# A recurrent block with a mixture-of-experts gate: biases put into PSUM by ScalarE, silu and half-tanh on ScalarE, experts in pairs, weights loaded in three groups

## What is computed

```python
xn = layernorm(x)
# the recurrent branch, on every second token of xn
xs = xn[:, ::2];  xs = xs * rsqrt(mean(xs**2) + 1e-6) * g_norm
x_proj, gate = split(xs @ w_in.T + b_in)
h = tanh(h * A + x_proj_t[:, None] * Bm)        # 2048 steps, h is (4, 512, 64)
y_t = h @ Cm.sum(0) + Dv * x_proj_t
s = repeat((y * silu(gate)) @ w_out.T + b_out, 2)
# the expert branch, on every token it needs (64 at a time per batch row)
spikes = sigmoid(xn @ W_enc + b_enc)            # 512 -> 1024
cont = spikes @ W_s2c + b_s2c                   # 1024 -> 64
gate2 = top-2 of softmax(cont @ Wr + br), renormalised      # 8 experts
eo = sum_e gate2_e * (relu(cont @ W1_e + b1_e) @ W2_e + b2_e)
spikes2 = sigmoid(eo @ W_c2s + b_c2s)           # 64 -> 1024
g = silu(layernorm(spikes2 @ W_dec + b_dec) * ln_g + ln_b)
out = x + s * g
```

## Time and profile before

| | |
|---|---|
| median of 3 runs | 6344.98 us |
| the profiled execution, its own time | 6343.27 us |
| its span, first to last instruction | 6341.6 us |
| PE busy | 6147.9 us, 97% |
| DVE busy | 5732.7 us, 90% |
| POOL busy | 5613.0 us, 89% |
| ACT busy | 3988.1 us, 63% |
| mean granted TensorE clock | 0.988 |
| DMA, mean over the span | 106 GB/s |

### The profile page before, as it was taken

How to read it: one execution, slowest core, us unless ns; L and a number is a source line. 1 busy time by engine, 2 the same in 40 slices (tenths; PEclk the granted TensorE clock), 3 DMA queues, 4 the chain that set the end, 5 groups by cost and what they waited for, 6 DMA issues and landing times.

```text
span 6341.6 us, 89178 instructions
## 1 busy us (share of the span) xinstructions
PE 6147.9 (97%) x29376; PEld 3202.8 (51%) x29376; DVE 5732.7 (90%) x10060; ACT 3988.1 (63%) x8390; POOL 5613.0 (89%) x3276
## 2 busy tenths in 40 slices
PE   5999999999999999999999999999999999999998
PEld 3555545555555455455554554555545545555554
DVE  4999999999999999999999999999999999999997
ACT  3666666666666666666666666666666666666665
POOL 4988989989889889899898898998988989989987
PEclk9999999999999999999999999999999999999999
DMA  5444444444434444444344444443444444444443
GB/s 144 104 110 99 110 105 104 110 102 107 110 99 110 105 103 110 102 107 112 97 110 106 103 113 102 105 113 95 109 108 102 114 101 106 112 96 110 109 102 80
DMA packets 157799, 672.95 MB, mean 106 GB/s; under 512 B 45589, under 2 KB 46613, under 8 KB 91799
## 3 DMA queue, kind: packets, MB, share of 16 engines
q1 hardware_dynamic: 157336, 667.24, 42.5%
HBM read 616.73 MB, written 50.33 MB: 105 GB/s over the span
## 4 chain that ended last, share of the span: by engine, by line
PE 91%; DVE 3%; POOL 3%; ACT 1%; issue 1%; SPq 1%; DMA 0%; POOLq 0%; DVEq 0%
PE bank L844 17%; PE bank L793 14%; PE ps_y L760 14%; PE ps_acc L856 9%; PE ps_acc L899 7%; PE bank L899 7%; PE bank L780 7%; PE bank L920 3%; PE bank L878 3%; PE bank L832 2%; POOL u L498 1%; PE bank L891 1%; PE ps_acc L891 1%; PE ps_acc L805 1%; PE ps_acc L878 1%
## 5 line engine op out<-in xcount | busy, mean ns | idle before, releaser
L498 POOL TENSOR_TENSOR u<-xb,bt 128x1024 f32<-128x1024 f32 x2048 | 4831.7, 2367 | 535.2 <-DVE ps_z L996 521.3
L600 ACT ACTIVATE h<-ps_z 128x512 f32<-128x512 f32 x4096 | 2377.1, 602 | 1280.0 <-DVE ps_z L996 1208.3
L990 DVE TENSOR_TENSOR ps_z<-h,ps_A 128x512 f32<-128x512 f32 x4096 | 2673.9, 691 | 416.0 <-ACT h L600 369.5
L996 DVE TENSOR_TENSOR ps_z<-ps_z,u 128x512 f32<-128x512 f32 x4096 | 2660.6, 691 | 8.7 <-POOL u L498 8.7
L844 PE MATMUL bank<-wide,w 65*128 65x256 f32 x4096 | 1138.8, 403 | 7.6
L760 PE MATMUL ps_y<-h,c_wide 128*32 128x512 f32 x8192 | 986.5, 599 | 0.0
L844 PEld LDWEIGHTS bank<-wide,w 65*128 65x128 f32 x4096 | 698.9, 189 | 454.6 <-issue 320.2
L793 PE MATMUL bank<-xnT,w_enc 128*128 128x256 f32 x4096 | 920.9, 383 | 6.5 <-ACT wide L623 6.5
L793 PEld LDWEIGHTS bank<-xnT,w_enc 128*128 128x128 f32 x4096 | 769.7, 190 | 213.0 <-issue 106.1
L681 ACT ACTIVATE hT<-bank 128x512 f32<-128x512 f32 x1024 | 604.1, 598 | 384.0 <-PE bank L844 366.6
L856 PE MATMUL ps_acc<-hT,w 128*64 128x256 f32 x4096 | 668.0, 404 | 6.7
(11 more groups left out here) (107 smaller groups left out, 4295.7 us busy)
## 6 DMA issues: line engine op xcount, KB each, us to landing
xb<-x_proj_scratch SPq DMA_DIRECT2D x2048, 256.0 KB, 4.5
xbuf<-in_L_attn_x SPq DMA_DIRECT2D x256, 128.0 KB
xres<-in_L_attn_x SPq DMA_DIRECT2D x512, 64.0 KB
out<-g SPq DMA_DIRECT2D x256, 128.0 KB
x_proj_scratch<-xp SPq DMA_DIRECT2D x256, 64.0 KB
w_in<-in_L_attn_w_in SPq DMA_DIRECT2D x1, 2048.0 KB
w_enc<-in_L_ffn_W_enc SPq DMA_DIRECT2D x1, 2048.0 KB
w_dec<-in_L_ffn_W_dec SPq DMA_DIRECT2D x1, 2048.0 KB
```

The costliest lines, as they stand in the source:

```text
L498: pool.tensor_tensor(u[:, tau % 2, :, :], xt, bt[:, :, :], ALU.mult).then_inc(u_ready, 1)
L600: act.activation(h[:, tau % RING, f, :], ps_z[:, f, :], ACT.Tanh).then_inc(h_ready, 1)
L990: dve.tensor_tensor(ps_z[:, f, :], h[:, (tau - 1) % RING, f, :], ps_A[:, f, :], ALU.mult).then_inc(m_done, 1)
L996: dve.tensor_tensor(ps_z[:, f, :], ps_z[:, f, :], u[:, tau % 2, f, :], ALU.add).then_inc(z_ready, 1)
```

## The change

- **Biases by ScalarE.** The three one-row matmuls of N=512 (decode twice, fin_out) go. ACT copies the bias, spread over 128 rows, into the bank (`dec_seed`, `out_seed`), and the matmuls add to it. The router's two bias matmuls and two copies go as well: Wr is turned into 64 columns of differences between experts, with the identity behind them, and one matmul for each half of the tokens makes both; one bias row of 256 columns is written before (`controller`).
- **Decode's layer norm.** W_dec and b_dec are centred once at the start, so that no mean is needed; ACT's Square with a sum gives the variance, and DVE's statistics, aggregates and centring go.
- **Sigmoids become tanh(x/2)**, with the affine part folded into the weights at the start. **Silu** runs on ACT alone, and POOL's three products go.
- **Routing** takes six smaller steps on DVE in place of eight; ACT's copy of the logits goes. The scale chain of the input norm is three small ACT and four small POOL operations in place of eight on POOL.
- **Experts in pairs**: two ups, then two downs, with four buffers for the relu's output in place of two.
- **Loads** in three groups on two queues: SyncE's (first) and ACT's (early, late), each waited for where it is needed. Preparing the weights is added at the start.
- Slots of the tables are moved throughout; `y` number 6 now stands between the two decodes.

The diff, cut to its core:

```diff
-PE_EXPERTS = (19, 19, 19, 19, 19, 19, 19, 19, 19, 19, 19, 20, 22, 22, 24, 28, 28)
...
+PE_EXPERTS = (19, 19, 19, 19, 19, 20, 22, 24, 28)
...
+        hidden = [hT[:, 0, :], hT[:, 1, :], conte_flat[:, 0:2 * T2], conte_flat[:, 2 * T2:4 * T2]]
...
+                sp.dma_start(dst, src).then_inc(first_loaded, 16)
...
-            def dec_silu(blk, q):
-                pool.wait_ge(g_sigmoid, 2 * blk + q + 1)
-                pool.tensor_tensor(g[:, q, :], g[:, q, :], sg[:, :], ALU.mult).then_inc(sg_used, 1)
...
+                act.wait_ge(p_stats_done, 4 * blk + 4)
+                act.activation(p_var[:, 0, :], p_mv[:, :, 1], ACT.Identity, bias=ln_eps[:, :])
+                act.activation(p_var[:, 1, :], p_mv[:, :, 1], ACT.Identity, bias=both_eps[:, :], scale=1.0 + RMS_EPS)
+                act.activation(p_mean[:, :], p_mv[:, :, 0], ACT.Copy, scale=-1.0).then_inc(p_moments, 1)
...
-            def gate_sig(blk, par):
+            def gate_silu(blk, par):
                 wait_drained(act, proj_fill(blk, FILL_WIN + 1))
-                if not is_first(blk):
-                    act.wait_ge(sg_used, sg_number(blk, None))
-                act.activation(sg[:, :], gt[:, par, :], ACT.Sigmoid).then_inc(gate_sigmoid, 1)
-            def sigmoids(src, k, bias):
+                act.activation(gt[:, par, :], gt[:, par, :], ACT.Silu).then_inc(gate_opened, 1)
+            def half_tanhs(src, k, bias):
                 for half in range(2):
                     m = 2 * k + half
                     ins = act.activation(wide[:, m, :], src[:, T2 * half:T2 * half + T2],
-                                         ACT.Sigmoid, bias=bias[:, m:m + 1])
+                                         ACT.Tanh, bias=bias[:, m:m + 1], scale=0.5)
...
+            def dec_seed(blk, q):
+                if q == 0:
+                    wait_drained(act, (blk, C2S_FILL[1]))
+                else:
+                    act.wait_ge(acc_drained, 2 * blk + 1)
+                act.activation(dec_out[q][:, :], b_dec_all[:, :], ACT.Copy).then_inc(dec_seeded, 1)
+            def out_seed(blk):
+                if is_first(blk):
+                    act.wait_ge(late_loaded, LATE)
+                wait_free(act, fin_fill(blk, FILL_FIN + 1))
+                act.activation(bank[1][:, :], b_out_all[:, :], ACT.Copy).then_inc(out_seeded, 1)
+            def dec_square(blk, q):
+                wait_dec_filled(act, blk, q)
+                if not (is_first(blk) and q == 0):
+                    act.wait_ge(d_stats_done, 2 * blk + q)
+                act.activation(squares[:, :], dec_out[q][:, :], ACT.Square,
+                               accum_out=d_ss[:, q:q + 1]).then_inc(d_stats_done, 1)
+            def dec_silu(blk, q):
                 wait_dec_drained(act, blk, q)
-                act.wait_ge(sg_used, sg_number(blk, q))
-                act.activation(sg[:, :], g[:, q, :], ACT.Sigmoid).then_inc(g_sigmoid, 1)
+                act.activation(g[:, q, :], g[:, q, :], ACT.Silu).then_inc(g_silu, 1)
...
+            load_early(w_enc[:, :, :], W_enc.rearrange("(k p) n -> p k n", p=P))
+            load_early(w_dec[:, :, :], W_dec.rearrange("(k p) n -> p k n", p=P))
+            load_early(w_s2c[:, :, :], W_s2c.rearrange("(k p) n -> p k n", p=P))
...
+            load_late(w_1[0:M, :, :], W1.rearrange("e m h -> m e h"))
...
+            act.wait_ge(first_loaded, FIRST)
...
+            act.wait_ge(early_loaded, EARLY)
...
+            act.wait_ge(weights_shaped, 1)
+            act.activation(w_dec_shift[:, :], w_dec_sum[:, :], ACT.Copy, scale=-0.5 / D).then_inc(weights_shaped, 1)
+            act.activation(w_s2c[:, :, :], w_s2c[:, :, :], ACT.Copy, scale=0.5)
...
+            act.wait_ge(weights_shaped, 2)
+            for k in range(KH):
+                ins = act.activation(w_dec[:, k, :], w_dec[:, k, :], ACT.Identity, bias=w_dec_shift[:, k:k + 1], scale=0.5)
+            ins.then_inc(weights_shaped, 1)
+            gate_silu(0, 0)
+            act.wait_ge(columns_summed, 1)
+            act.activation(cont_bias[0:M, :], ps_acc[0:M, 8:9], ACT.Identity, bias=cont_bias[0:M, :]).then_inc(biases_shifted, 1)
+            act.wait_ge(biases_shifted, 2)
...
+                pe.matmul(ps_acc[:, T2:T2 + 2 * (E * E + M)], ones[96:97, :], br_row, start=True, stop=True)
                 for k in range(KH):
                     half = k % 2
                     ins = pe.matmul(contT_acc[M * half:M * half + M, :], w_s2c[:, k, :], wide[:, k, :],
-                                    start=(k < 2), stop=(k >= KH - 2))
+                                    start=False, stop=(k >= KH - 2), skip_group_check=True)
...
-                    pe.matmul(logit_acc[:, q, :], ones[64:65, :], bias_rows[64:65, 0:E], start=True, stop=False)
-                    pe.matmul(logit_acc[:, q, :], tokens, w_r[:, :], start=False, stop=True)
-                    ins = pe.matmul(cont_acc[:, q, :], tokens, ident_2[:, :], start=True, stop=True)
+                    ins = pe.matmul(routed[:, q, :], tokens, w_r[:, :], start=False, stop=True,
+                                    skip_group_check=True)
...
-            def experts(blk, n):
-                if n < 16:
-                    expert_up(blk, n)
-                if n > 0:
-                    expert_down(blk, n - 1)
+            def experts(blk, p):
+                if p < 8:
+                    expert_up(blk, 2 * p)
+                    expert_up(blk, 2 * p + 1)
+                if p > 0:
+                    expert_down(blk, 2 * p - 2)
+                    expert_down(blk, 2 * p - 1)
...
-                if q == 0:
-                    wait_free(pe, (blk, FILL_DEC))
-                else:
-                    pe.wait_ge(acc_drained, 2 * blk + 1)
+                pe.wait_ge(dec_seeded, 2 * blk + q + 1)
                 dst = dec_out[q]
-                pe.matmul(dst[:, :], ones[0:1, :], bias_rows[0:1, :], start=True, stop=False)
...
-                wait_free(pe, at)
-                pe.matmul(bank[1][:, :], ones[32:33, :], bias_rows[32:33, :], start=True, stop=False)
+                pe.wait_ge(out_seeded, blk + 1)
...
+            pe.wait_ge(weights_shaped, 3)
+            for k in range(KH):
+                pe.matmul(ps_acc[0:M, 8:9], w_s2c[:, k, :], ones[:, 0:1], start=(k == 0), stop=(k == KH - 1))
+            for k in range(KH):
+                ins = pe.matmul(ps_y[:, :], ones[:, :], w_dec[:, k, :], start=(k == 0), stop=(k == KH - 1))
+            ins.then_inc(columns_summed, 1)
...
-                        dve.tensor_tensor(atleast[:, q], others[:, q], own[:, q], ALU.is_ge)
-                        ins = dve.tensor_tensor(over[:, q], others[:, q], own[:, q], ALU.is_gt)
+                        ins = dve.tensor_tensor(ahead[:, q], lead[q], least[:, :, :], ALU.is_ge)
...
+                if n == 3 or n == 4:
+                    q = n - 3
+                    ins = dve.tensor_tensor(ahead[:, q], lead[q],
+                                            sel[:, q].unsqueeze(1).to_broadcast([P, E, E]), ALU.mult)
                 if n == 5:
-                    ins = dve.tensor_tensor(selected, logit_acc, sel[:, :, :], ALU.mult)
-                if n == 6:
-                    ins = dve.tensor_reduce(top_sum[:, :], selected, AX.X, ALU.add)
-                if n == 7:
-                    ins = dve.scalar_tensor_tensor(out=margin, in0=logit_acc, scalar=2.0,
-                                                   in1=top_sum[:, :].unsqueeze(2).to_broadcast([P, 2, E]),
-                                                   op0=ALU.mult, op1=ALU.subtract)
+                    ins = dve.tensor_reduce(behind[:, :, :], ahead[:, :, :, :], AX.X, ALU.add)
...
-                dve.bn_stats(d_st[:, q, :], dec_out[q][:, :]).then_inc(d_stats_done, 1)
...
-                dve.scalar_tensor_tensor(out=v, in0=v, scalar=d_mv[:, q, 0:1], in1=ln_g_all[:, :],
-                                         op0=ALU.subtract, op1=ALU.mult).then_inc(d_centred, 1)
...
+                dve.scalar_tensor_tensor(out=v, in0=v, scalar=d_r[:, q:q + 1], in1=ln_g_all[:, :],
+                                         op0=ALU.mult, op1=ALU.mult).then_inc(d_scaled, 1)
...
+                ins = dve.tensor_tensor(g[:, q, :], dec_out[q][:, :], ln_b_all[:, :], ALU.add)
...
+            dve.wait_ge(early_loaded, EARLY)
+            dve.tensor_reduce(w_dec_sum[:, :], w_dec[:, :, :], AX.X, ALU.add).then_inc(weights_shaped, 1)
...
+            dve.scalar_tensor_tensor(out=b_dec_all[:, :], in0=ps_y[:, :], scalar=b_dec_sum[:, :], in1=b_dec_all[:, :],
+                                     op0=ALU.add, op1=ALU.add).then_inc(biases_shifted, 1)
```

384 lines of the change are left out of this document (190 added, 194 removed).

## The result

The change makes the kernel faster: 6140.9 us median (6129.2 to 6168.1) against 6346.6 for the kernel before in the same session, ratio 0.968 (95% interval 0.965 to 0.971). That is 206 us less, where 346 were forecast; the forecast of 6000 us was 141 us too low, inside its range. The profiled execution took 6143.1 us, its span 6141.3. The four executions, fastest first, had a mean granted TensorE clock of 0.987, 0.985, 0.985 and 0.980.

What follows compares the result with a forecast made beforehand. PE was taken to set the pace, handed to DVE through ACT. PE 90.9 and DVE 90.3 with friction 1.1 gave 92.0 us a block, 5.4 less, 346 in all, ends 0: about 6000 us, range 5890 to 6180.

Steps and rivals of the forecast that it cites:

- ACT's order binds: Rival, chance 0.20: uncovered seeds and norm steps delay tanhs, experts cost their full 3.2; 96.2 us a block, 6267, half 6133.
- the friction: Block's sum: PE and DVE locked at semaphores, slower expert pairs not fully made up; 1.1 us a block, bounds 0 to 3.2.
- the clock: PE's short clock fall in the matmuls behind the router goes as the router's thin stretch is halved; gain 0.55 us a block.
- PE's side: PE's block after savings on bias matmuls, router, expert pairs and clock: 97.4 falls to 90.9 us, wait of 1.36 included.
- DVE's side: DVE's block without decode statistics and some routing steps: busy 89.5 falls to 87.3 us, some 89.0 with idle between steps.
- What ACT adds: New seeds and squares on ACT: second decode seed and first square delay tanhs, 1.3 us a block, making DVE 90.3.
- The cover that I named for the output's copy: Output seed on ACT stands beside DVE's shift; if such cover is missing, the other new pieces cost up to 2.1 more.
- tables are switched: Rival, chance 0.01: silu and tanh share no table, so three silus add 7.7 us of loads a block; again 6450.
- Both ends: Start and tail: start net +3 (-10 to +12), tail -3 from a bias matmul and two POOL products; together 0.
- No friction: Rival, chance 0.20: PE alone binds and the downs save their full 1.1; 90.3 us a block, 5890 us.
- The clock falls in the decode: Rival, chance 0.03: PE waits at `y` between the decodes, second decode runs at 1.2 GHz; 99.1 us a block, 6452.
- Nothing comes of it: Rival, chance 0.01: whatever PE saves, it waits for DVE; that asks for a DVE side of 97.

Runs made afterwards that it cites:

- the relu's kernel: Changed kernel with the thirteenth relu moved one step later, behind the tanhs of step 20: 6029.3 us, ratio 0.950.
- the projection's run: Changed kernel with ACT emptying the second transpose's bank before the two tanhs of step 9, not between them: 6142.7 us, ratio 0.969.
- the late loads: Changed kernel with the late group of loads issued by SyncE's queue and no longer by ACT: 6141.7 us, ratio 0.968.
- the pairs with a hole: Changed kernel, experts in pairs, with ACT's copy of the second bias moved behind one more tanh (14.0 to 14.5): 6466.3 us, ratio 1.019.
- the shift's run: Changed kernel with the second decode's scale and shift on DVE, and the POOL step before them, one step earlier: 6137.6 us, ratio 0.967.
- single experts without the hole: Changed kernel with experts one by one and ACT's copy of the second bias ahead of both relus (14.0 to 13.5): 6240.7 us, ratio 0.984.
- the bias rows: Changed kernel with the three bias rows again added by PE matmuls and ACT's three copies taken out: 6214.7 us, ratio 0.980.
- the single experts with the hole: Changed kernel with the experts one by one again, ACT's copy of the second bias left at 14.0: 7369.8 us, ratio 1.162.
- the run of all moves: Changed kernel with relu, second bias copy, square, evacuation, scaling and late loads all moved together: 6029.4 us, ratio 0.951.

## Why the prediction was right and wrong

The measured 6141 us lies inside the range of 5890 to 6180, but outside 5930 to 6080, which the forecast's own story allowed. The wider range held it because it took in half of the rival *ACT's order binds*, 6133. So the direction and the sums of work were right by reasoning, and that the time fell inside is in part luck: two terms of the block's sum were off, the friction and the clock.

**PE's side** (90.9 with a wait of 1.36, so 89.5 of work). Right: 89.2 busy in a block at full clock, 88.8 in the relu's kernel. Its parts held too: three bias matmuls 2.8 (3.15 forecast), experts in pairs 2.4 (2.2, bounds 1.7 to 2.8), and the eight passes behind the router take 3.70 to 3.84 us in block after block, as in the shorter blocks before.

**The clock** (0.55 a block booked as gained) is the first step that failed. I took the fall to go because the router's thin stretch is halved. It came one piece earlier instead, in the controller, and cost 0.57 us a block. In every run with PE's wait of 1.33 us there (the changed kernel, the projection's run, the late loads, the pairs with a hole) it comes right behind that wait, in half of the blocks or more; with the wait gone (the shift's run) it comes behind the wait of 1.65 us that took its place; with a wait of 1.1 us (single experts without the hole), of 0.4 (the relu's) or none (the bias rows) it doesn't come at all. In the kernel before, it came in the last matmuls of this stretch with no wait in front, so a wait isn't its only way; what sets it off wasn't tested by itself.

**DVE's side**. 87.3 busy forecast, 87.8 measured.

**What ACT adds** (1.3). The second copy made DVE wait 0.56 us and the first square 0.37: 0.93, and taking both away gave 0.46 because PE was next (88% of the chain). The cover that I named for the output's copy held. The new silus take 0.62 and 0.67 us, and the whole run has two loads of a table, both before the first step, the second just ahead of the first silu. Silus and tanhs follow each other from there without another, so *tables are switched* is out:

```profile
L666 ACT ACTIVATE g<-g 128x512 f32<-128x512 f32 x128 | 79.6, 622 | 0.0
L577 ACT ACTIVATE gt<-gt 128x512 f32<-128x512 f32 x64 | 43.1, 673 | 0.0
L661 ACT ACTIVATION_READ_ACCUMULATOR squares<-bank 128x1 f32 x64 | 13.1, 204 | 0.0
L703 ACT ACT_TABLE_LOAD x1 | 1.3, 1283 | 21.5 <-issue 21.5
L577 ACT ACT_TABLE_LOAD x1 | 1.3, 1283 | 0.0
```

**The friction** (1.1, bounds 0 to 3.2) is the second step that failed, and the larger: at full clock the block came to 93.4 and not 92.0. With the clock's 0.57 that is 2.0 us a block, 127 us in 64 blocks. I had spread it over seven pairs at 0.45 each, and argued that PE enters the experts a step ahead of the relus, so that little of it shows. A pair takes 2.94 us, as forecast. But the head start is used up by the `y` between two pairs, and then one relu in the wrong place holds one tanh for 1.8 us. Moving it alone gave 92.10, what I had forecast, and DVE's waits that are left at the experts (0.32, 0.44, 0.36 and 0.21 us) are near my 1.1; that term was a choice between bounds, so the agreement is partly luck. A reading of the order of ACT beside the order of PE would have found it: the relu that is due behind the `y` was the one to look at, not the mean of all pairs.

**Both ends** (0). The first sum of a step comes at 91.61, 8.0 later than before, where I had +3; the last `y` is added 22.0 us from the end, before 24.5. I expected ACT to be held by its loads until about 40; it was 50. One load, of the experts' second biases (the second `w<-in_L_ffn_b`), held its queue for 17.7 us, where the same load had taken 7.8 on SyncE's queue before the change:

```profile
29.36 0.77 ACTq L677 DMA_DIRECT2D w<-in_L_ffn_W  x1
30.16 17.73 ACTq L677 DMA_DIRECT2D w<-in_L_ffn_b  x1
...
50.86 1.28 ACT L703 ACT_TABLE_LOAD   x1 [21.54 <-issue]
```

That is 5 or 6 us, and the one long fall in the profiled run 12.5: with the 127 of the blocks 145 of the 146 us by which the profiled execution (6143, forecast 5997) was slower. Long falls I had nowhere in the sum.

**The rivals.** *No friction*, 90.3 a block, wasn't reached by any run: the lowest block was 91.64, of which 88.9 is PE's work and 2.7 its waits for ACT and DVE. Two runs moved these waits about without a shorter block; that they can't be removed isn't shown. *ACT's order binds* was the right mechanism at about half its size (2.0 of 4.2 us a block, the clock's part included), by a relu and not by the seeds and norm steps that I had named. *The clock falls in the decode* had the right mechanism in the wrong place: the clock does fall, in the experts; one block in 64 in the profile of the kernel as built, one in three with one copy half a step later, and then the change is slower than no change. I had given it 0.03, on the ground that waits of 2.1 us had been harmless before. They had been, at their place; here a wait of 1.33 us at the controller had a short fall behind it in every second block. *Nothing comes of it* is excluded.

**Signs named ahead.** Clock 1.00 behind the router: nearly, but in half of the blocks it fell one piece ahead. Pairs near 3.0 us: 2.94. No table load: yes. PE's idle time of 2 or 3 us: 4.3. DVE's wait for tanh halved: from 5.8 to 4.3 only. First step near 85: 91.6.

## What to carry to other kernels

When two engines come close to the same pace, ask of each in-order engine between them which single instruction is due behind something that may be late; one such place was worth 112 us here, and no sum of mean times shows it. A wait that moves on when its cause is removed, with the block as long as before, is slack: follow the recurrence (who waits last, in every block) and not the largest number in the list of waits. Before a schedule is judged, look at the granted clock of each stretch, since a hole of half a microsecond of TensorE at one place cost some ten times its own length. And when falls of the clock differ from run to run, compare the blocks without one before calling a move worth nothing.

## What the runs showed of the hardware

**The clock falls without an idle stretch, and not every time.** In the long block of the changed kernel PE worked 5.99 of 6 us before and through the fall:

```profile
2200.00:2206.00 6.00, 5.99 (x26) 3.48 (x26) 5.48 (x10) 5.29 (x11) 4.97 (x4) 0.84 0.41 102
2206.00:2212.00 6.00, 6.00 (x17) 3.63 (x18) 3.66 (x7) 2.67 (x5) 4.64 (x2) 0.50 0.34 74
2224.00:2230.00 6.00, 6.00 (x22) 2.56 (x25) 2.99 (x5) 2.17 (x4) 3.86 (x2) 0.50 0.00 0
```

PE's nearest wait of over 0.15 us ended 7.6 us before the fall and was 0.34 long. The same order of work ran at 1.00 through the experts of the blocks beside it. All long falls of the 14 profiles but those of the single experts with the hole begin at the first downs of the experts or the bias ahead of them (the start and the end of a run, with falls of 3 to 14 us, left aside). The clock stayed at 0.50 for 24 to 27 us, with the single experts for 31 to 38; a single fall lengthened its block by 11 to 13 us. In the run of all moves long falls come exactly 12 blocks apart. With a hole at `w` of 1.87 us every block fell, with 0.47 every third, and without one between none and five in 64. By the Trainium skill (TensorE: Matmul & The Clock Gate, Part 1: The HAM clock gate) the clock is set by how busy TensorE has lately been, judged at times that run free of the kernel; falls at a fixed number of blocks agree with that. The same section of the Trainium skill ties a fall to TensorE being idle, and here it fell while TensorE was busy.

**Open.** What decides whether an undisturbed block falls wasn't settled: moving the `y`, widening the margin at `w` and moving PE's waits didn't stop it, and a hole of 0.54 us one pair of ups earlier brought two falls in 64 blocks where 0.47 us at `w` brought 22. Each count is from one profiled execution. The first block fell in some kernels and not in others. With 91.64 us a block, each fall less would be worth 13 us. Nor was it shown what decides which of two blocks gets the short fall.

**One small load can hold a queue.** The load of the experts' second biases (`b2`, 8 rows of 64, 2 KB) took ACT's issuing queue 17.7 us, and 20.2 us when it was issued on SyncE's; the load of `W2` just ahead of it took 0.8. In the kernel before it took 7.8. Another load of biases (`b_enc`, 4 KB) took ACT's queue 12.4 us, before 3.5 on SyncE's. Whether its shape or the traffic ahead of it holds the queue wasn't tested. With the late loads on SyncE's queue ACT's first instruction came 26 us sooner and the first sum of a step 15.
